# State-space convolution and gated recurrence on one core: the first unit's sums move to other memory, y's load moves forward in the queue, and the first units are prepared one group sooner

## The reference

```python
# x: (8, 2048, 512) float32
x = x + layernorm(gelu(conv(layernorm(x), K) + D * layernorm(x)))     # K: state-space kernel of B, C, P, Q, diag, step
# then a gated recurrence, whose time axis is the batch of 8 and whose batch is the 2048 rows
x_ = layernorm(x)
for xt in x_:                                   # 8 steps
    ft = sigmoid(xt @ wf.T + c @ uf.T + bf)
    it = sigmoid(xt @ wi.T + c @ ui.T + bi)
    gt = tanh(xt @ wc.T + c @ uc.T + bc)
    c = ft * c + it * gt                        # c starts as in_c, the same for all rows
h = tanh(x_ @ wo.T + c @ uo.T + bo)
x = x + layernorm(h)
```

## Time and profile before

| | before |
|---|---|
| median of 3 runs | 2779.64 us (2774.74 to 2779.66) |
| the profiled execution's own time | 2779.75 us |
| its span | 2777.9 us |
| PE busy | 2591.0 us (93%) |
| DVE busy | 1941.2 us (70%) |
| ACT busy | 1511.5 us (54%) |
| POOL busy | 959.8 us (35%) |
| mean granted PE clock | 0.972 |

### The profile page before, as it was taken

The page is one execution under the profiler, slowest core; times in us unless marked ns, Lnnn a source line. Parts: engine busy times, 40 slices in busy tenths (PEclk is TensorE's granted clock), DMA queues, the critical chain, the costliest instruction groups (busy, mean ns, idle before and its releaser), DMA issues.

```text
span 2777.9 us, 54870 instructions
## 1 busy us (share of the span) xinstructions
PE 2591.0 (93%) x21507; PEld 2101.9 (76%) x21507; DVE 1941.2 (70%) x3404; ACT 1511.5 (54%) x2802; POOL 959.8 (35%) x1449
## 2 busy tenths in 40 slices
PE   4499999996799999999998989999999999999998
PEld 4277877884588888888886878888888888644443
DVE  7865666546776767776777777777677765478778
ACT  6655556564555555555555555555555554345444
POOL 7777676622221222121222222212221210144445
PEclk9799999997899999999999999999999999999999
DMA  9878787788445534543554564455355434288777
GB/s 329 290 222 292 261 287 243 259 308 273 121 107 131 124 100 109 133 121 96 118 139 124 113 169 100 106 130 127 96 109 138 116 96 111 95 295 282 263 255 265
DMA packets 524548, 489.94 MB, mean 176 GB/s; under 512 B 275584, under 2 KB 406912, under 8 KB 519040
## 3 DMA queue, kind: packets, MB, share of 16 engines
q1 hardware_dynamic: 524288, 486.43, 59.5%
HBM read 270.60 MB, written 150.73 MB: 152 GB/s over the span
## 4 chain that ended last, share of the span: by engine, by line
PE 80%; DVE 8%; DMA 4%; ACT 3%; issue 2%; POOL 1%; SPq 1%; DVEq 0%; POOLq 0%; ACTq 0%
PE bank L1909 28%; PE bank L1919 27%; PE bank L1977 12%; PE bank L1749 3%; PE bank L1799 3%; PE bank L1785 2%; PE bank L1807 2%; DVE big L1432 2%; PE bank L1961 1%; DMA big<-yd 1%; PE bank L1761 1%; DMA big<-big 1%; DMA big<-xr 1%; DVE big L1344 1%; PE bank L1769 1%
## 5 line engine op out<-in xcount | busy, mean ns | idle before, releaser
L1909 PE MATMUL bank<-big 128*128 128x256 f16 x8064 | 1098.5, 276 | 73.0 <-ACT big L1156 29.2
L1919 PE MATMUL bank<-big 128*128 128x256 f16 x7056 | 965.3, 273 | 0.0
L1909 PEld LDWEIGHTS bank<-big 128*128 128x128 f16 x8064 | 796.3, 99 | 184.4 <-ACT big L1156 32.4
L1919 PEld LDWEIGHTS bank<-big 128*128 128x128 f16 x7056 | 691.7, 98 | 81.1
L883 POOL TENSOR_SCALAR big<-big 128x1 f32<-128x1 f32 x256 | 55.7, 217 | 1308.5 <-DVE big L1456 785.4
L1977 PE MATMUL bank<-big 128*128 128x512 f16 x1536 | 332.2, 379 | 0.0
L1137 ACT ACTIVATE big<-big 128x512 f32<-128x512 f32 x384 | 290.9, 805 | 62.4 <-DVE big L1626 61.9
L1626 DVE TENSOR_TENSOR big<-bank,big 128x512 f32<-128x512 f32 x192 | 131.4, 684 | 228.4 <-PE bank L1919 218.2
L1977 PEld LDWEIGHTS bank<-big 128*128 128x128 f16 x1536 | 150.3, 98 | 181.2
L1050 ACT ACTIVATE big<-big 128x512 f32<-128x512 f32 x256 | 206.6, 807 | 116.3 <-POOL big L885 115.5
L1172 ACT ACTIVATE big<-bank 128x512 f32<-128x512 f32 x192 | 113.9, 593 | 260.8 <-PE bank L1919 251.8
(11 more groups left out here) (209 smaller groups left out, 3594.2 us busy)
## 6 DMA issues: line engine op xcount, KB each, us to landing
big<-xr SPq DMA_DIRECT2D x16, 2048.0 KB, 11.1
big<-xg SPq DMA_DIRECT2D x64, 512.0 KB, 6.7
big<-kpad SPq DMA_DIRECT2D x32, 1024.0 KB, 12.4
yd<-big SPq DMA_DIRECT2D x16, 2048.0 KB, 17.3
big<-x SPq DMA_DIRECT2D x128, 256.0 KB, 3.2
x1d<-big SPq DMA_DIRECT2D x128, 256.0 KB, 2.0
xtd<-big SPq DMA_DIRECT2D x64, 512.0 KB, 4.9
big<-xtd SPq DMA_DIRECT2D x64, 512.0 KB, 4.5
```

Of the source, the lines that this page charges most:

```text
L1909: ins = e.matmul(o, WX[2 * g + lw][:, q, kt, 128 * a:128 * a + 128], slot[u % 2][:, part, lx, k0 + kt, :], start=(first and kt == 0 and (l ...
L1919: ins = e.matmul(o, WC[2 * g + lw][:, q, kt, 128 * a:128 * a + 128], cc[unit(u)[1] % 2][:, qc, lx, kt, :], start=False, stop=end, skip_gro ...
```

## The change

It has four parts. `xs0`, the sums of unit 0, move out of y's memory into the convolution's constants (`keep`) and the head of the small inputs (`acc`), which are no longer in use; so y's load for unit 1 waits only for unit 0's additions (`x1`), and stands ahead of the loads of x. `bias0` moves behind DVE's additions and the first sums. In `prepare`, y's load for the next unit and the two loads of x ahead of it now stand ahead of turns 8v+4 and 8v+5. And the stages of unit 1 are each one group earlier, those of unit 2 too except the last.

```diff
@@ prep_schedule
-            places = ((1, 2, 3, 4, 5, 5), (6, 7, 8, 9, 10, 10), (11, 12, 13, 14, 15, 15), (16, 17, 18, 19, 20, 20))[v - 1]
+            places = ((0, 1, 2, 3, 4, 4), (5, 6, 7, 8, 9, 10), (11, 12, 13, 14, 15, 15), (16, 17, 18, 19, 20, 20))[v - 1]
@@ memory
-        xs0 = [f32(m0_at + 512 * r, 512) for r in range(4)]
+        xs0 = [f32(keep + 512 * r, 512) for r in range(3)] + [acc]
@@ load_y
-                w.wait_ge(s["ss"], 8 * v)
-                w.wait_ge(s["fb"], 20)
-                w.wait_ge(s["xh"], 8 * v - 2)
-                w.wait_ge(s["xlo"], 8 * v - 2)
+                w.wait_ge(s["x1"], 4 * v)
+                if v > 1:
+                    w.wait_ge(s["ss"], 8 * v)
+                    w.wait_ge(s["xh"], 8 * v - 2)
+                    w.wait_ge(s["xlo"], 8 * v - 2)
@@ SP, prepare
                 if stage == 5:
-                    for k in range(2, 6):
-                        turn(8 * v + k)
+                    turn(8 * v + 2)
+                    turn(8 * v + 3)
                     if v + 1 < NU:
                         load_x1(v + 1, 0)
                         load_x1(v + 1, 2)
                 if stage == 6:
                     if v + 1 < NU:
                         load_y(v + 1)
-                    turn(8 * v + 6)
-                    turn(8 * v + 7)
+                    for k in range(4, 8):
+                        turn(8 * v + k)
@@ SP, ahead of the groups
             load_y(0)
-            for c in CHUNKS:
+            for c in CHUNKS[:2]:
                 load_x1(0, c)
             w.wait_ge(s["accs"], 16 * 3)
             e.dma_start(fbs, accd.rearrange("g p h -> p g h")).then_inc(s["accs"], 16)
+            for c in CHUNKS[2:]:
+                load_x1(0, c)
...
+            load_y(1)
             for c in CHUNKS:
                 load_x1(1, c)
-            load_y(1)
             w.wait_ge(s["w_lo"], low_base(8))
             w.wait_ge(s["wd"], stored(7))
-            w.wait_ge(s["fb"], 12)
+
+            w.wait_ge(s["fb"], 20)
@@ DVE, row_sums and the opening
-                    w.wait_ge(s["x1"], 4)
+                    w.wait_ge(s["accs"], 16 * 3)
...
-            w.wait_ge(s["fb"], 12)
-            e.tensor_tensor(bias0, bank[0][:, 0:12].rearrange("p (g m) -> p g m", g=3), bias, ADD).then_inc(s["yc"], 1)
             for n in range(4):
                 add(n)
             row_sums(0, 0)
+            w.wait_ge(s["fb"], 12)
+            e.tensor_tensor(bias0, bank[0][:, 0:12].rearrange("p (g m) -> p g m", g=3), bias, ADD).then_inc(s["yc"], 1)
             low(0)
```

## The result

| | before | changed |
|---|---|---|
| median | 2779.65 us (4 runs, 2774.74 to 2779.93) | 2748.31 us (4 runs, 2747.06 to 2751.82) |
| span of the profiled execution | 2777.9 us | 2747.1 us |
| mean granted PE clock | 0.972 | 0.977 |
| PE busy | 2591.0 us | 2581.0 us |

The medians differ by 31.3 us. The ratio of the times on record, which comes with a 95% interval, is 0.9897 (0.9883 to 0.9911), and that is 28.6 us (25 to 33). On another chip the same kernel took 2752.0 us against 2777.8, 25.8 us less.

A forecast was written before the change was run, and what follows sets the result against it. PE's gaps, set by y's load, DVE's statistics to low parts, and the last transpose, were taken as the bound. Terms 8.4 + 4.1 + 6.4 + 2.7 = 21.6 us off 2779.75 gave 2758.2 us, range 2750 to 2768.

The forecast's parts named there:

- What bounds the kernel: PE busy 93% of the span; gains only in its gaps, where units 1 and 2 wait for y's load, DVE, transposes.
- The opening: Unit 0: with the constant term moved, additions and what follows start 4.4 us sooner, first group at about 640.5.
- y's load for unit 1: Lands at 645.3, between 644.1 and 646.5, so DVE's statistics start then in place of 651.73.
- Unit 1's chain: First statistics to last low part, then transposes: low parts end at 677.0, unit 1 starts at 685.4, 8.4 us sooner.
- up to 1.5 us: Unit 1's first sums wait for stores behind the weights' loads; allowed for in the range, none in the sum.
- The four transposes behind y's load: Four in place of two follow y's load before unit 1; y lands at 681.8, the fourth transpose at 685.7.
- Unit 2's chain: Takes 42.2 us from y's landing to last low part; unit 2 starts at 734.0, 12.5 us sooner, another 4.1.
- Two of the signs of being wrong: Wrong if DVE's stretch from statistics to last low part isn't shorter than 33 us for unit 1 or 43 for unit 2.
- The two stalls behind: PE's waits at 803.48 and 854.80: loads for units 4 and 5 go 3.2 us sooner each, together 6.4 us.
- Units 15 and 17: Later units without state products: y's load is issued 1.35 us sooner at each, together 2.7 us.
- The order brings nothing: Rival: a filled queue makes y land when it did, only the opening counts; 2767.3, or 2770 to 2772 us; chance 0.14.
- The slower one: Rival: y's load for unit 1 caught in the full queue; landing at 675 would give 2788 us; chance 0.03.

The follow-up runs named there:

- weights_late: Changed kernel with three of six state-weight loads and unit 0's stores of its turned input moved behind unit 1's first two x1 stores: 2749.49 us, ratio 0.9895.
- order put back: Changed kernel with y's load put back behind turns 8v+4 and 8v+5: 2764.77 us, ratio 0.9954.
- order_only: Kernel before with only y's load for the next unit, with two loads of x, moved ahead of turns 8v+4 and 8v+5: 2762.63 us, ratio 0.9942.
- y_behind_weights: Changed kernel with y's load for unit 1 issued behind the six loads of the state weights: 2764.8 us, ratio 0.9953.

## Where the prediction was right in its steps, and where its sizes were off

- **What bounds the kernel** was right: the chains from y's load through DVE and the last transpose set units 1 and 2, and nothing changed between groups 23 and 84, where PE is full (the changed kernel is 25.5 us ahead at both).
- **The opening**, 4.4 us, was over-sized: unit 0's first group starts at 642.40, 2.5 us sooner, and the constant term's place is worth only 0.3 to 1.6 us at the end. The first addition comes at 623.83, as forecast (623.5). But POOL, which I took to be busy "for a moment", became the bound: its eight rates run back to back from 621.68 to 634.3.
- **y's load for unit 1** was right: 644.71 for 645.3. It took 7.0 us, so the row's 6.7 was the better guide, and not the 4.4 worked out from the Trainium skill (DMA: Bandwidth & Descriptors, "Anatomy of one DMA"). That section's fit is for DMAs issued from GpSimd, and this load is issued from SP, which the prediction doesn't say.
- **Unit 1's chain**, 8.4 us, measured 6.4. The step that failed is the one kept out of the sum, "up to 1.5 us" for the first sums' wait for stores behind the weights; it was 3.97, and weights_late wins it back. The low parts end at 678.95, where 677.0 was forecast. The four transposes behind y's load cost what they should: y lands at 684.14 and the unit starts 3.25 us later, where the sum has 3.6 (681.8 to 685.4, though it writes 3.4 when it comes to unit 2).
- **Unit 2's chain**: 12.5 us forecast for its start, 11.05 measured, 4.6 of them beyond unit 1's 6.4, for 4.1. By group 11 the ledger has 13.4. Most of this is PE's clock: in the kernel before, the granted clock is 0.51 over the 3.74 us from 746.50 on (a window shown below), 1.8 us lost, and in the changed kernel it is 1.00 from 735.45 on. The rest is a short wait. The changed kernel's second trace runs unit 2's second product slowly too, in 1.46 us in place of 0.83, so this part isn't the same in every run.
- **Two of the signs of being wrong came true.** DVE's stretch from the first statistics to the last low part was to be shorter than 33 us for unit 1 and 43 for unit 2, and it is 34.2 (644.71 to 678.95) and 43.2 (684.14 to 727.30). For unit 1 it would be 30.3 without the 3.97 us of the store. For unit 2 the saving of 2.4 us in the waits of its last group wasn't had in full: 42.2 was worked out. The start was 1.45 us later than forecast all the same, and not more, since y's load for unit 3 took 6.7 us in place of the 8.0 in the sum.
- **The two stalls behind**, 6.4 us, were under-sized most: groups 11 to 23 win 12.1 us. The step that failed is that a stall's wait is all that it costs, so that 4.03 and 3.62 were upper limits. In the kernel before, PE's clock falls behind both stalls. Windows of that kernel, at unit 2's start and behind each stall:

```profile
746.50:750.24 3.74, 3.74 (x18) 2.69 (x19) 2.33 (x6) 1.81 (x3) 2.88 (x8) 0.51 1.05 322
803.48:810.00 6.52, 6.52 (x45) 5.22 (x46) 5.94 (x11) 3.92 (x8) 2.58 (x7) 0.74 0.16 62
857.53:863.36 5.83, 5.83 (x30) 4.24 (x31) 5.42 (x11) 3.24 (x6) 3.29 (x8) 0.55 0.26 93
```

  The mean granted clock is between its levels of 1.2 and 2.4 GHz because each stretch holds both. PE is busy throughout, so 3.74 x 0.49 = 1.8 us are lost at unit 2's start, 6.52 x 0.26 = 1.7 behind the first stall and 5.83 x 0.45 = 2.6 behind the second. PE's products behind the stalls, before:

```profile
804.83 1.49 PE L1909 MATMUL bank<-big 128*128 128x256 f16 x6
...
808.44 0.82 PE L1919 MATMUL bank<-big 128*128 128x256 f16 x6
...
857.53 1.46 PE L1909 MATMUL bank<-big 128*128 128x256 f16 x6 [1.06 <-ACT big L1165]
```

  So the first stall cost 4.03 + 1.7 = 5.7 us, and all of it is gone. The second cost 3.62, a short wait of 1.06 behind it and the 2.6, and a wait of 1.25 is left of it: 6.0. That is 11.8 of the 12.1. Behind the waits of 1.36 (order put back) and 1.25 the clock doesn't fall.

  What took the first stall away is y's load for unit 4. It was issued 3.2 us sooner as forecast, and it also landed in 6.7 us in place of 9.7; the 6.2 us of the ledger at group 16 are this same gain seen on DVE. With the order put back the load took 7.0 us, 2.7 less than before; the wait is less by as much, 1.36 for 4.03, and the clock stays up. So 4.3 of the first stall's 5.7 us hang on the 9.7 us of one trace, and why that load took so long stays open. At group 21 come 3.7 us, at group 23 2.6 more.
- **Units 15 and 17**, 2.7 us, measured 5.3. The issue is 1.35 us sooner as forecast, but the landing is shorter too, by 1.2 us at unit 15 (8.1 to 6.9) and 0.9 at unit 17 (7.2 to 6.3). The step that failed is that the row's landing time was kept although what stands ahead of the load changed.
- **The rivals.** "The order brings nothing" was refuted by order_only. The slower one is real, 12.8 us in y_behind_weights, but not met in this order of issue. By the ledger, units 1 and 2 brought 13.4 us where 12.5 were forecast, the stalls 12.1 for 6.4, and units 15 and 17 5.3 for 2.7: 30.8 for 21.6. The chains that were named are the ones that moved. What the prediction left out is the clock behind a stall, which adds 4.3 us at the two stalls and 1.8 at unit 2's start, and it had unit 1's start too large by 2.0. So the errors partly cancel in the total.
- **What no run took back.** The ledger gives the order 14.4 to 15.7 us, the stages' places 6.7 to 8.0 and the constant term's place 0.3 to 1.6, each put back alone. Of the 29.8 to 31.1 some 6 to 8 are left to y's early load for unit 1, with the sums' new memory that allows it, and to what the parts give only together. No run takes that load back alone.

## What to carry to other kernels

Where an engine works in order and the first thing in a stage waits for a load, count the load's issue as well as its transfer: here two transposes of 1.29 us each on the issuing queue, moved behind the load, were worth some 15 us, at the early units and at units 15 and 17. A stall on PE can cost more than its wait: behind waits of 4.03 and 3.62 us the granted clock fell and 1.7 and 2.6 us went on top, while behind waits of 1.25 and 1.36 us it stayed up. So look at the granted clock behind a stall before pricing its removal. If one load in a trace takes 9.7 us where its like take 7 to 8, a second trace tells whether that is the kernel's or that run's. And when a load moves forward in a full queue, look for what now waits at its end: here a small store behind 6.4 MB, which cost 4 us of wait. The wait went away when over half of that traffic was issued behind the first two stores.

## What the runs showed of the hardware

POOL's small scale operations take longer while an addition of DVE runs beside them. Before, the third operation of each of the first four rates (L885) took 0.26 or 0.27 us, with DVE idle or at small statistics; in the changed kernel, where DVE runs additions at the same time, the same operation takes 0.59 to 0.66 in four of the first five rates, and a rate comes every 1.77 us in place of 1.38. It isn't that one operation: in the kernel before, where DVE's additions fall beside the second operation of rates 5 to 7 (L884), it is this one that takes 0.86 us in place of 0.56 to 0.58. Beside DVE's statistics, which have one input, both keep their time: the 0.57 us at 625.11 run beside statistics from 624.56 to 625.25. POOL, changed kernel:

```profile
624.81 0.22 POOL L887 TENSOR_SCALAR big<-big 128x1 f32<-128x1 f32 x1 [0.15 <-POOL big L889]
625.11 0.57 POOL L888 TENSOR_TENSOR big<-big 128x1 f32<-128x1 f32 x1
625.78 0.64 POOL L889 TENSOR_SCALAR big<-big 128x1 f32<-128x1 f32 x1
626.58 0.21 POOL L887 TENSOR_SCALAR big<-big 128x1 f32<-128x1 f32 x1 [0.15 <-POOL big L889]
626.88 0.56 POOL L888 TENSOR_TENSOR big<-big 128x1 f32<-128x1 f32 x1
627.54 0.66 POOL L889 TENSOR_SCALAR big<-big 128x1 f32<-128x1 f32 x1
```

The Trainium skill (GPSIMD Engine Reference, "Specifications") says that POOL's interfaces to SBUF are shared with VectorE and that instructions of DVE with two SBUF inputs contend; the additions here have two, so the trace agrees, but no run isolated it.
